# Centring two batches on POOL, and a new order of the queues from the last q on

## The reference

```
y   = layernorm(x)
q   = y @ Wq.T + bq ; k, v = ctx @ Wk.T + bk, ctx @ Wv.T + bv          # 16 heads of 16
corr = irfft(rfft(q) * conj(rfft(k))).mean(over the head's 16)          # 512 delays
w, delays = top_k(corr, 6) ; w = softmax(w)
out = sum over the 6 of w * (v rolled by its delay)
x   = x + out @ Wo.T + bo
z   = layernorm(x)
h   = bitlinear(z, w1, b1) ; h = gelu(h) ; x = x + bitlinear(h, w2, b2)

bitlinear(x, w, b): xq = round(rmsnorm(x) * 127 / max|.|) per row,
                    wq = -1, 0 or 1 per weight times mean|w| ; xq @ wq.T + b
```

## Time and profile before

| | us |
|---|---|
| median of 3 runs | 150.09 (149.57 to 150.13) |
| the profiled execution | 149.76 |
| its span in the trace | 148.2 |
| PE, DVE, ACT, POOL busy | 137.3, 122.4, 94.2, 85.1 |
| granted clock of TensorE, share of full | 0.997 |

### The profile page before, as it was taken

How to read it: one execution, slowest core, us unless ns; L and a number is a source line. 1 busy time by engine, 2 the same in 40 slices (tenths; PEclk the granted TensorE clock), 3 DMA queues, 4 the chain that set the end, 5 groups by cost and what they waited for, 6 DMA issues and landing times.

```text
span 148.2 us, 2497 instructions
## 1 busy us (share of the span) xinstructions
PE 137.3 (93%) x737; PEld 94.7 (64%) x742; DVE 122.4 (83%) x316; ACT 94.2 (64%) x188; POOL 85.1 (57%) x152
## 2 busy tenths in 40 slices
PE   6769979999999999999999998999899699999881
PEld 2444679566936487667777884668467456666770
DVE  1759997999999989344978799998999989798971
ACT  4023695696632315122223957999999999999980
POOL 3025229978903850599490262995980574938681
PEclk9999999999999999999999999999999999999998
DMA  4999999900980079000000039106476899989933
GB/s 153 314 346 358 385 349 373 258 9 0 159 124 0 0 112 170 10 1 2 0 7 0 0 71 156 20 4 122 83 113 131 155 199 157 219 169 195 203 111 106
DMA packets 30321, 19.80 MB, mean 134 GB/s; under 512 B 17122, under 2 KB 29283, under 8 KB 30308
## 3 DMA queue, kind: packets, MB, share of 16 engines
q1 hardware_dynamic: 26084, 15.45, 38.6%
q0 software_dynamic: 4224, 4.19, 19.6%
HBM read 9.40 MB, written 2.10 MB: 78 GB/s over the span
## 4 chain that ended last, share of the span: by engine, by line
PE 54%; ACT 20%; issue 10%; DMA 5%; POOL 4%; DVE 3%; SPq 1%; POOLq 0%; ACTq 0%; DVEq 0%
PE psum L487 16%; PE psum L500 9%; PE psum L431 9%; PE psum L590 7%; DMA wkv<-in_wkv_t 5%; ACT prod L840 4%; ACT x_f L840 4%; ACT wf L831 4%; ACT xq L821 3%; PE psum L514 3%; PE psum L603 3%; PE psum L474 2%; ACT xn L813 2%; ACT xc_and_least L805 2%; POOL hr L1433 1%
## 5 line engine op out<-in xcount | busy, mean ns | idle before, releaser
L487 PE MATMUL psum<-wkv,c_f 128*128 128x512 f32 x56 | 25.4, 594 | 0.0
L742 ACT COPY kv_f<-psum 128x512 f32<-128x512 f32 x16 | 9.4, 585 | 20.7 <-PE psum L487 17.0
L1212 DVE TENSOR_REDUCE hmax<-wf 128x1 f32<-128x1025 f32 x16 | 19.4, 1217 | 1.7 <-ACT wf L831 1.6
L649 PE MATMUL psum<-w2q,kv_f 128*128 128x256 f16 x128 | 16.5, 273 | 1.7 <-ACT kv_f L852 0.7
L621 PE MATMUL psum<-w1q,xq_t 128*128 128x512 f16 x64 | 16.4, 379 | 1.4 <-issue 1.4
L831 ACT ACTIVATE wf<-psum,xdeq 128x1024 f32<-128x1024 f32 x16 | 17.6, 1118 | 0.0
L487 PEld LDWEIGHTS psum<-wkv,c_f 128*128 128x128 f32 x56 | 10.3, 190 | 10.2 <-issue 10.0
L649 PEld LDWEIGHTS psum<-w2q,kv_f 128*128 128x128 f16 x128 | 11.9, 98 | 5.9 <-DMA kv_f<-kv_f 1.3
L500 PE MATMUL psum<-wq,x_f 128*128 128x256 f32 x64 | 15.1, 381 | 0.0
L603 PE MATMUL psum<-wo,out_t 128*128 128x256 f32 x64 | 14.8, 382 | 0.0
L590 PE MATMUL psum<-fold_signal,out_f 128*128 128x256 f32 x64 | 14.7, 381 | 0.0
(11 more groups left out here) (166 smaller groups left out, 317.8 us busy)
## 6 DMA issues: line engine op xcount, KB each, us to landing
ctx_in<-in_ctx SPq DMA_DIRECT2D x4, 512.0 KB, 7.5
res<-in_x SPq DMA_DIRECT2D x4, 512.0 KB, 7.4
res<-bo_all POOLq DMA_DIRECT2D x4, 512.0 KB, 7.2
res<-b_all POOLq DMA_DIRECT2D x4, 512.0 KB, 6.0
out<-res SPq DMA_DIRECT2D x16, 128.0 KB, 2.3
wf<-in_w_t SPq DMA_DIRECT2D x1, 1024.0 KB, 8.5
wf<-in_w_t SPq DMA_DIRECT2D x2, 512.0 KB, 10.4
wkv<-in_wkv_t SPq DMA_DIRECT2D x1, 512.0 KB, 7.2
```

What stands on the lines that cost most here:

```text
L487: mm = pe.matmul(bank(K_BANKS + ft), c_f[:, c, ft * P:(ft + 1) * P], wkv[:, c, :], start=(c == 0), stop=(c == NC - 1))
L649: mm = pe.matmul(psum[:, Y_BANKS + t % 2, 0:D], hq_t[:, t % HQ, k, :], w2q[:, k, :], start=(k == 0), stop=(k == NK - 1))
L1212: dve.tensor_reduce(hmax[:, j:j + 1], hid_and_least[j], AX.X, ALU.max, apply_absolute_value=True).then_inc(s["hmax_made"], 1)
```

## The change

ACT's `centre(2)` and `centre(3)` go; POOL gets `centre_by_pool(n)` for these two batches, one tensor_scalar instruction per tile with the same result. Batches 0 and 1 stay on ACT. From the last q spectrum on, the calls of all five queues stand in another order; what each call does is unchanged. `project(0, half)` gets a wait for DVE's last products, which the order had implied. The diff, cut to its core (of the order, the parts that the text below speaks of):

```diff
+            def centre_by_pool(n):
+                pool.wait_ge(s["res_added"], n * 2 + 2)
+                pool.wait_ge(s["xc_made"], n)
+                if n > 1:
+                    pool.wait_ge(s["xq_made"], n - 1)
+                    pool.wait_ge(s["xss_made"], n - 1)
+                    pool.wait_ge(s["xmax_made"], n - 1)
+                for a in range(NA):
+                    ins = pool.tensor_scalar(xc[:, n % 2, a, :], res[:, n, a, :], -float(D), row_sum[:, n % 2, a:a + 1], ALU.mult, ALU.add)
+                ins.then_inc(s["xc_made"], 1)
...
@@ PE @@
                 if n:
                     pe.wait_ge(s["res_added"], n * 2 + (half - 1))
+                else:
+                    pe.wait_ge(s["prod_used"], 2 * NB - 1 + half)
...
             project(0, 1)
+            inverse(1, 0)
             turn_g(1)
-            inverse(1, 0)
             inverse(1, 1)
...
             up(2)
-            up(3)
             project(2, 0)
             project(2, 1)
+            up(3)
             inverse(3, 0)
             inverse(3, 1)
             up(4)
...
             down(1)
-            down(2)
+            turn_h(5)
             up(8)
             up(9)
-            turn_h(5)
+            down(2)
             down(3)
             up(10)
...
@@ DVE @@
             choose(1)
-            weigh(1)
             add_residual(0, 0)
             add_residual(0, 1)
+            weigh(1)
+            row_max(0)
             combine_g(1)
-            row_max(0)
...
             hidden_max(4)
+            hidden_max(5)
+            h_inverse(4)
+            x_deq(2)
+            h_inverse(5)
             add_residual(3, 0)
-            h_inverse(4)
             quantise_h(4)
-            hidden_max(5)
             add_residual(3, 1)
-            x_deq(2)
             hidden_max(6)
+            quantise_h(5)
             finish(0)
...
```

More of the change, by code:

```diff
@@ L866, in _ @@
             inverse_copy(2, 0)
+            gelu(0)
             square_x(1)
-            gelu(0)
+            inverse_copy(2, 1)
             gelu(1)
-            inverse_copy(2, 1)
-            square(0)
             gelu(2)
             round_x(1)
+            square(0)
             square(1)
+            square(2)
             gelu(3)
-            square(2)
+            inverse_copy(3, 0)
             square(3)
-            inverse_copy(3, 0)
-            centre(2)
             inverse_copy(3, 1)
@@ L883, in _ @@
             gelu(5)
+            square(4)
+            square(5)
             round_x(2)
-            square(4)
             gelu(6)
-            square(5)
-            centre(3)
+            square(6)
             gelu(7)
+            square(7)
             square_x(3)
-            round_x(3)
             gelu(8)
             quantise_h(6)
-            square(6)
+            round_x(3)
             gelu(9)
             copy_h(5)
-            square(7)
             gelu(10)
-            copy_h(7)
             square(8)
             gelu(11)
+            square(9)
             gelu(12)
-            square(9)
+            square(10)
+            copy_h(7)
             quantise_h(10)
-            square(10)
+            square(11)
+            gelu(13)
+            gelu(14)
             copy_h(9)
-            gelu(13)
-            square(11)
-            gelu(14)
             square(12)
+            gelu(15)
             copy_h(11)
-            gelu(15)
             square(13)
+            square(14)
             copy_h(13)
-            square(14)
+            square(15)
             copy_h(14)
-            square(15)
             copy_h(15)
@@ L1265, in _ @@
             add_residual(2, 0)
+            h_inverse(1)
+            h_inverse(2)
             x_deq(1)
             add_residual(2, 1)
+            quantise_h(1)
+            quantise_h(2)
             hidden_max(3)
[L1269 to L1272, removed]
             inverse_out(3, 0)
+            h_inverse(3)
             row_max(2)
@@ L1488, in _ @@
             aug_parts(1)
+            centre_by_pool(2)
             h_rms(0)
-            h_rms(1)
             h_deq(0)
             add_b2(1)
+            h_rms(1)
             h_deq(1)
+            x_rms(2)
             h_rms(2)
+            h_deq(2)
             h_rms(3)
-            h_deq(2)
+            aug_parts(2)
             h_deq(3)
-            x_rms(2)
-            aug_parts(2)
+            centre_by_pool(3)
             h_rms(4)
+            h_deq(4)
             h_rms(5)
             x_rms(3)
-            h_deq(4)
             aug_parts(3)
+            h_rms(6)
             h_deq(5)
-            h_rms(6)
             h_deq(6)
             h_rms(7)
+            h_deq(7)
             add_b2(2)
-            h_deq(7)
             h_rms(8)
+            h_rms(9)
             h_deq(8)
-            h_rms(9)
             h_rms(10)
```

90 lines of the change are left out of this document (44 added, 46 removed).

## The result

The changed kernel takes 151.41 us (median of 10 runs, 149.64 to 153.11) against 149.95 (10 runs, 149.28 to 150.53). The ratio of comparable runs is 1.0068, interval 1.0035 to 1.0101: slower, where 148.3 was forecast (ratio 0.988). In the changed kernel three runs, all over 1.5 % above its fastest at an unchanged clock (0.999 to 1.000) and all with over 2.4 us outside the span, are left out of the ratio as slow, and with them the ratio of the means is 1.0099. The profiled execution took 152.1 with a span of 149.6.

The account below looks back on a forecast made before the run. ACT was taken as the bound from about 90 us: 3.19 + 0.15 - 1.05 - 0.15 - 0.15 = 2.0 saved, less 0.2 for unseen waits, leaves 1.8. Forecast 148.3 us, own range 147.3 to 149.2, 8 in 10 147.0 to 150.6.

Parts of the forecast that it names:

- The premise: From about 90 us ACT, with 10.00 us of work in each 10, is the bound; PE and DVE stand close behind.
- step 4: Batch 2's transposes: round_x(2) later, at 111.0, but aug out at about 113.9, landing at 116.9, so up(8) earlier than 118.54.
- step 1: Stretch of batch 0: inverse(1,0) ahead of turn_g(1) on PE brings up(0) to 91.05 for 91.22, 0.15 gained.
- step 2: ACT's new start: gelu(0) ahead of square_x(1), pm(2,1) ahead of gelu(1), both waiting for PE; 1.05 us lost.
- steps 3 and 5: POOL's centring of batches 2 and 3 ready at 105.3 and 116.5, just in time for square_x(2) and square_x(3); 0.15 idle at batch 2.
- The rival of the dear centring: POOL's centring instructions cost 0.82 to 0.90 each, so ACT waits before square_x(2) and square_x(3): 150.5 to 151.1; chance 0.13.
- Given back by DVE: Rival: three quantise_h on DVE each wait 0.53 for a POOL centring instruction, leaving 0.2 gained: 149.9; chance 0.19.
- Step 6: From batch 3 on, same ACT work bar waits of 0.1 to 0.2; square(15) ends at 141.1, last finish starts at 143.35.
- The prediction's own sign of being wrong: Forecast wrong if ACT's total idle from 90 us is over 2.5 (one of three such signs).
- Outside the span: Time of the execution around the trace's first to last event, taken over unchanged from the kernel before: 1.6 us.

Follow-up runs that it names:

- early parts: The changed kernel with aug_parts(2) on POOL right behind h_rms(2), ahead of h_deq(2) and h_rms(3): ratio 1.0011 (0.9984 to 1.0037).
- the old order: The kernel before, its order kept, with only the centring of batches 2 and 3 moved from ACT to POOL: 150.66 us, ratio 1.004.
- all put together: The changed kernel with ACT's start as before, round_x(2), round_x(3), aug_parts(2), up(8), batch 3's x transpose and row_max(3) moved earlier: 151.17 us, ratio 1.0059.
- The second version with this DMA early: The changed kernel with b2 DMAs of batches 1 to 3 one place earlier and round_x(2), x_deq(2), aug_parts(2), up(8) forward: 156.43 us, ratio 1.046.

## Why the prediction was wrong

**The premise.** "ACT is the bound" was read from ten tenths. A full row says that ACT never waits; it doesn't say that nothing else ends at the same time. PE was idle for only 0.44 before up(8), and up(8) ended 0.04 before gelu(8) began: with PE's queue as it was, whatever ACT did, gelu(8) could come at most 0.5 earlier. I used that row in step 4, but only as something to be moved, not as a bound on what a faster ACT can give. By it alone the forecast would have been at most 0.5 for all that ACT saves ahead of gelu(8), unless step 4 delivers. With 2.4 of ACT's work left out the runs gave nothing (0.9999; gelu(8) 28.85 after up(0) for 28.81).

**Step 4** then was what all hung on, and it failed: up(8) at 118.50 for 116.9. Two queues came late to it, and both let aug out only at 115.1 to 115.3, where 113.9 was forecast. On ACT round_x(2) ran at 112.06 for 111.0, from two terms. up(0) came at 91.41 for 91.05; step 1's 0.15 can't be told from the scatter, since other profiles of this PE order have up(0) at 90.3 to 91.7. And aug_parts(1) ended at 103.6 for 102.3: DVE's quantise_h(1) and (2) now stand ahead of hidden_max(3), right behind add_residual(2,1), and meet the last two of the four small instructions, 0.45 and 0.38 longer; so up(4), which waits for these parts, came at 106.18 for 105.56, and gelu(4) and gelu(5) behind it. bring_x(2) then held SP's queue from 113.78 to 115.0. On POOL x_deq(2)'s result of 111.9 lay until 114.21, behind h_rms(2), h_deq(2) and h_rms(3). Moving POOL's part alone (early parts) changed nothing, as ACT's and SP's was as late.

| | predicted | measured |
|---|---|---|
| one centring instruction | 0.53 | 0.47 and 0.57 |
| square_x(2), square_x(3) | 105.3, 116.7 | 105.91, 118.03 |
| ACT's new waits, step 2 | 1.05 | 1.03 |
| round_x(2) | 111.0 | 112.06 |
| up(8) | 116.9 | 118.50 |
| square(15) ends | 141.1 | 144.24 |
| last finish | 143.35 | 146.73 |
| outside the span | 1.6 | 1.5 or 2.5 |

**Steps 2, 3 and 5** were right in the waits, the price and the two covers that "just last", though the times of steps 3 and 5 came 0.6 and 1.3 later. The rival of the dear centring had the price wrong, and its mechanism (ACT in front of square_x(3)) shows in the old order, 2.16 us, and with all put together, 0.57, but not in the change. Two of its arguments need setting right. The two instructions of the 1802 ns row don't start 1.2 apart but at 26.29 and 38.13 (1.27 and 2.34 long); 1.2 lies between each and the one ahead of it. And the section of the Trainium skill that it names (GPSIMD Engine Reference, 4.1) gives twice VectorE's time for two-input operations and calls one-input ones roughly line-rate; the trace agrees with that, 0.47 against the 0.41 of DVE's two-input instruction of this size. "Given back by DVE" named the wrong place: what DVE's quantise_h lengthened were POOL's small instructions. The Trainium skill (SBUF — State Buffer, "Who interferes with whom") has the second to come fully blocked, and the trace agrees in both directions (0.21 to 0.66 on POOL beside quantise_h; 0.81 for four columns on DVE); I applied it to the long instructions and forgot the short ones, where a wait of 0.4 brings 0.2 to 0.6.

**Step 6** put 0.15 into the sum for up(11) and up(12). They were 0.38 and 1.11: round_x(3) behind gelu(8) and quantise_h(6), and batch 3's transposes behind it, which in this execution also landed late. At gelu(8) the changed kernel had 0.5 us less left to do on ACT (square(6) and square(7) done, 2.08, and round_x(3) not, 1.59); it ends 0.7 later (square(15) at 144.24 for 143.53). That PE takes over the end from POOL was right (0.23 before the last finish). The prediction's own sign of being wrong, ACT idle for over 2.5 from 90 us on, came true at 3.6.

**Outside the span** was taken over from before, as was done for every term that "can't change". It is somewhat under half of the loss.

What stays open: how the 0.68 of span divides between the new start, POOL's queue and round_x(3) with the late landing behind it. The edits that undo the start or lighten POOL's queue land between 1.001 and 1.003 with their share of late loads in them, and their intervals overlap with each other and with the change's own.

## What to carry to other kernels

Before a saving on a full engine is counted, find where it reads another engine's result. How long that result had been ready, plus how long the other engine had been idle before making it, caps the gain up to there as long as the other engine's queue stays as it is (here 0.04 and 0.44); a test that leaves the work out (three centring instructions of four, ratio 0.9999) tells it in one run. In a tightly laid-out kernel an order found for all engines stands or falls as a whole: parts of it alone cost 0.4 to 8 %. Compare the span and the time outside it apart. And compare rows of two traces from a common event on: here the start of the stretch alone scattered by 0.8.

## What the hardware showed that I had not expected

**A small DVE instruction shut out for 6 us.** In the version with the b2 DMA of batch 1 earlier, DVE and then POOL in order of time:

```profile
93.33 5.96 DVE L1161 TENSOR_SCALAR xscale<-xinv 128x4 f32<-128x4 f32 x1
```

```profile
91.44 1.27 POOL L1487 DMA_DIRECT2D res<-b_all  x1 [2.71 <-ACT xc_and_least L805]
92.21 1.58 POOL L1413 TENSOR_TENSOR m_a<-kv_f,g_re 128x512 f32<-128x512 f32 x1
93.23 1.57 POOL L1414 TENSOR_TENSOR m_b<-kv_f,g_im 128x512 f32<-128x512 f32 x1
...
97.50 1.75 POOL L1424 TENSOR_TENSOR out_f<-m_c,m_d 128x512 f32<-128x512 f32 x1
```

It takes 0.81 in the earlier trace rows and lasts here to 99.29, just behind the end of the last of six POOL instructions (99.25); these start 1.0 to 1.2 apart but show 1.56 to 1.75 each, so that one overlaps the next. PE then waited 4.73 for DVE's out_t, and after this wait the granted clock was 0.70 between 100 and 110. The second version with this DMA early shows the same (5.96, 4.75, 0.72). The wait and the lower clock fit the 5 %; why the DMA lets it come to this isn't shown.

**A transpose behind a 512 KB DMA.** Tile transposes land 3.2 to 3.3 us after their issue in the kernel before (the least and the median of nine). In the version with batch 3's transposes first, the one issued 0.4 behind POOL's b2 DMA took 7.2.

**Instruction loads count.** One load of 16 KB that starts behind the 8 KB one, after the last store, adds some 0.9 us to an execution (2.41 to 2.61 for 1.48 to 1.65), and nothing in the span shows it. The queues' kinds in the trace do.
